# Eight of 32 value parts computed inside the attention steps, and setup work moved off the head of a differential-attention and mixture-of-experts kernel

## What is computed

```python
Q, K = xn @ Wq + bq, xn @ Wk + bk          # 16 heads, two halves of 64 each
V = xn @ Wv + bv                           # 16 heads x 64 = 1024 columns
P = softmax(Q1 K1^T / 8) - lam * softmax(Q2 K2^T / 8)
Y = concat(P V) @ Wo + bo                  # then a layer norm with gamma, beta, times 0.2
main = gelu(xn @ W1m + b1m) @ W2m + b2m    # the shared expert
# routing: per batch, the mean token picks the top 2 of 8 experts
ffn = a * main + (1 - a) * sum(gate_k * expert_k(xn))
```

## Time and profile before

| | |
|---|---|
| median of 3 runs | 1177.49 us (1175.26 to 1177.57) |
| the profiled execution's own time | 1176.92 us |
| its span in the trace | 1175.1 us |
| PE / DVE / ACT / POOL busy | 1128.0 / 904.8 / 949.8 / 979.9 us |
| mean granted TensorE clock | 0.991 of full speed |

### The profile page before, as it was taken

The page is one execution under the profiler, slowest core; times in us unless marked ns, Lnnn a source line. Parts: engine busy times, 40 slices in busy tenths (PEclk is TensorE's granted clock), DMA queues, the critical chain, the costliest instruction groups (busy, mean ns, idle before and its releaser), DMA issues.

```text
span 1175.1 us, 27816 instructions
## 1 busy us (share of the span) xinstructions
PE 1128.0 (96%) x9730; PEld 779.9 (66%) x9730; DVE 904.8 (77%) x1573; ACT 949.8 (81%) x1711; POOL 979.9 (83%) x609
## 2 busy tenths in 40 slices
PE   5899999999999999999999999999999999998998
PEld 4666666666666666666666666666666666664797
DVE  7878888888888888888888888888888888874510
ACT  3288899888898888898888898888898988885432
POOL 2589999999999999998888999999898888899000
PEclk9999999999999999999999999999999999998999
DMA  8942222222211222122212211222222212100000
GB/s 196 344 115 61 48 63 61 61 61 62 53 42 44 61 61 56 45 78 56 55 46 56 50 35 37 56 56 56 56 56 56 56 45 56 43 5 1 1 19 18
DMA packets 76439, 71.28 MB, mean 61 GB/s; under 512 B 43380, under 2 KB 65396, under 8 KB 76404
## 3 DMA queue, kind: packets, MB, share of 16 engines
q1 hardware_dynamic: 75396, 70.65, 23.1%
q10 hardware_dynamic: 880, 0.19, 0.1%
q0 software_dynamic: 128, 0.01, 0.0%
HBM read 22.59 MB, written 14.68 MB: 32 GB/s over the span
## 4 chain that ended last, share of the span: by engine, by line
PE 63%; ACT 20%; issue 6%; POOL 6%; DVE 4%; ACTq 1%; DMA 0%; DVEq 0%; SPq 0%; POOLq 0%
PE ps L567 20%; PE ps L535 18%; ACT work L753 11%; PE ps L553 10%; PE ps L489 8%; ACT p_mix L753 6%; POOL p_mix L448 3%; PE ps L652 3%; ACT pt L766 3%; PE ps L639 2%; POOL work L445 2%; PE ps L516 1%; DVE small L947 1%; DVE pt L903 1%; ACT small L719 0%
## 5 line engine op out<-in xcount | busy, mean ns | idle before, releaser
L947 DVE TENSOR_REDUCE small<-ps 128x1 f32<-128x1024 f32 x512 | 614.3, 1220 | 168.3 <-PE ps L535 168.3
L448 POOL TENSOR_TENSOR p_mix<-p_mix,work 128x1024 f32<-128x1024 f32 x256 | 608.8, 2378 | 21.4
L766 ACT ACTIVATE pt<-ps 128x512 f32<-128x512 f32 x512 | 306.8, 599 | 131.8 <-PE ps L553 129.7
L553 PE MATMUL ps<-ident,p_mix 64*128 64x64 f32 x4096 | 353.1, 227 | 5.6 <-POOL p_mix L448 2.8
L445 POOL TENSOR_SCALAR work<-work,small 128x1024 f32<-128x1024 f32 x256 | 307.4, 1201 | 50.4 <-DVE small L972 48.3
L553 PEld LDWEIGHTS ps<-ident,p_mix 64*128 64x128 f32 x4096 | 305.6, 139 | 55.9 <-issue 37.2
L753 ACT ACTIVATE p_mix<-ps,small 128x1024 f32<-128x1024 f32 x256 | 286.5, 1119 | 16.7 <-DVE small L947 16.7
L753 ACT ACTIVATE work<-ps,small 128x1024 f32<-128x1024 f32 x256 | 285.1, 1114 | 0.1
L567 PE MATMUL ps<-pt,v_h 128*64 128x512 f32 x1024 | 250.2, 610 | 0.7 <-ACT pt L766 0.7
L535 PE MATMUL ps<-k_hi,q_hi 64*128 64x512 f32 x512 | 227.5, 444 | 5.9 <-ACT p_mix L753 3.4
L535 PE MATMUL ps<-k_hi,q_lo 64*128 64x512 f32 x512 | 225.8, 441 | 0.0
(11 more groups left out here) (135 smaller groups left out, 1211.0 us busy)
## 6 DMA issues: line engine op xcount, KB each, us to landing
qx_hi<-q_hi SPq DMA_DIRECT2D x64, 256.0 KB, 3.8
qx_lo<-q_lo SPq DMA_DIRECT2D x64, 256.0 KB, 4.6
v_scratch<-pt SPq DMA_DIRECT2D x16, 512.0 KB, 5.4
v_h<-v_scratch SPq DMA_DIRECT2D x32, 256.0 KB, 3.1
w_scratch<-wqk_hi SPq DMA_DIRECT2D x16, 160.0 KB, 1.8
w_scratch<-wqk_lo SPq DMA_DIRECT2D x16, 160.0 KB, 1.9
wqk_hi<-w_scratch SPq DMA_DIRECT2D x16, 160.0 KB, 2.2
wqk_lo<-w_scratch SPq DMA_DIRECT2D x16, 160.0 KB, 2.3
```

Of the source, the lines that this page charges most:

```text
L448: pool.tensor_tensor(e1, e1, e2, ALU.add).then_inc(mix_done, 1)
L553: mm = pe.transpose(pt_ps[:, c * D:(c + 1) * D], p_mix[rows, col:col + P], ident[rows, rows])
L766: act.activation(pt4[:, kb % 2, :, j * P + half * D:j * P + (half + 1) * D], pt_ps.rearrange("p (c q) -> p c q", c=KC), ACT.Copy).then_inc ...
L947: dve.tensor_reduce(neg_max[:, m:m + 1], slot[SLOT[k, s]], AX.X, ALU.max, negate=True)\
```

## The change

It computes 24 value parts in the head and the last eight in attention steps 0, 1, 2, 4 and 5. Of the 24, every fourth (u % 4 = 3, six parts) is copied by ACT, and POOL adds the bias in SBUF. Parts 0 and 1 are computed ahead of the second `turn_x`. The wait on `v_stored` is split: step 3 waits for tiles 0 to 3 and 8 to 11, step 7 for tiles 4 to 7 and 12 to 15. SP issues `load_v(0, 0, 0)` after tile 11, the store of tile 15 after `prepare(1)`, and the expert weights after `prepare(2)`. `set_main` moves to POOL's steps 129, 130, 132, 133, 137 and 138. `start_y` moves behind `split_w(1)`. In steps 0 to 7 the reciprocals come ahead of the second row maximum.

```diff
+MAIN_AT, INPUT_AT = 129, (132, 133, 137, 138)
+V_LATE = {0: (24, 25), 1: (26, 27), 2: (28, 29), 4: (30,), 5: (31,)}
+V_EARLY = 24
...
+        def by_act(u):
+            return u < V_EARLY and u % 4 == 3
+        def v_out(u):
+            count = sum(by_act(w) == by_act(u) for w in range(u + 1))
+            return (v_copied if by_act(u) else v_evac), count
+        def v_place(u):
+            if u < V_EARLY + 2:
+                return 4 + (u + 2) % 4
+            return 6 if u in (26, 28) else 7
...
-            for i in range(NT):
-                sp.wait_ge(v_evac, 2 * i + 2)
+            def store_v(i):
+                for u in (2 * i, 2 * i + 1):
+                    if by_act(u):
+                        sp.wait_ge(v_added, u // 4 + 1)
+                    else:
+                        sp.wait_ge(*v_out(u))
                 sp.dma_start(v_scratch[i, :, :], v_st[:, i % TB, :]).then_inc(v_stored[i % TB], 16)
+
+            for i in range(V_EARLY // 2):
+                store_v(i)
                 if i % 2 and i // 2 < NW:
                     store_w(i // 2)
                     load_w(i // 2 + 2)
...
             for v in v_stored:
-                sp.wait_ge(v, 16 * B)
+                sp.wait_ge(v, 16)
             load_v(0, 0, 0)
+            for i in range(V_EARLY // 2, NT - 1):
+                store_v(i)
+            def load_experts():
...
             for n in range(1, IT):
                 prepare(n)
+                if n == 1:
+                    store_v(NT - 1)
+                if n == 2:
+                    load_experts()
+                if n == IT // B - 2:
+                    for v in v_stored:
+                        sp.wait_ge(v, 16 * B)
...
-            start_y()
             for n in range(1, NW):
                 split_w(n)
-            set_main()
+            pool.wait_ge(xn_ready, 2 * B)
+            start_y()
+            def bias_v(first, end):
+                for u in range(first, end, 4):
+                    pool.wait_ge(*v_out(u))
+                    hv = u % 2
+                    pool.tensor_tensor(v_part(u), v_part(u), bv_bc[:, hv * BANK:(hv + 1) * BANK], ALU.add)\
+                        .then_inc(v_added, 1)
+            bias_v(3, V_EARLY)
...
+                set_main(n)
                 set_expert(n)
...
-            pe.wait_ge(v_evac, 2 * NT)
...
+                    if isinstance(g, int) and g * BODY + k == LAG:
+                        pe.wait_ge(*v_out(28))
...
+                    if isinstance(blk, int) and blk == 0:
+                        pe.wait_ge(*v_out(2 * NT - 1))
...
+                    if isinstance(g, int) and (g, k) == (0, 1):
+                        pe.wait_ge(*v_out(V_EARLY - 2))
+                        pe.wait_ge(*v_out(V_EARLY - 1))
...
+                if isinstance(g, int) and g == 0:
+                    for u in V_LATE.get(k, ()):
+                        values(u)
...
+                if isinstance(n, int) and (n, w) == (1, 1):
+                    act.wait_ge(v_mm, 2 * NT)
...
-                if half == 0 and isinstance(g, int) and g * BODY + k == LAG:
-                    for v in v_stored:
+                if half == 0 and isinstance(g, int) and g * BODY + k in (LAG, LAG + QB):
+                    for v in v_stored[kb * QB:(kb + 1) * QB]:
                         act.wait_ge(v, 16 * B)
...
-            evac_v(20, 2 * NT)
+            evac_v(20, V_EARLY)
...
-                if j == 1 and now(g, k, 1):
+                soon = isinstance(g, int) and g == 0 and k < TB
+                if (j == 1 or soon and j != 3) and now(g, k, 1):
                     inv_sums()
...
-                if j in (0, 2) and now(g, k, 1):
+                if j in (0, 2) and not soon and now(g, k, 1):
                     inv_sums()
+                if isinstance(g, int) and g == 0:
+                    for u in V_LATE.get(k, ()):
+                        evac_v(u, u + 1)
```

More of the change, by code:

```diff
@@ L144, in build @@
         wv_split, v_mm, v_evac = sem("wv_split"), sem("v_mm"), sem("v_evac")
+        v_copied, v_added = sem("v_copied"), sem("v_added")
         v_stored = [sem(f"v_stored{i}") for i in range(TB)]
@@ L203, in slot_free, with v_free, v_part, v_bank @@
             return exp_done, 2 * (g * BODY + k) + what + 1
+        def by_act(u):
+            return u < V_EARLY and u % 4 == 3
+        def v_free(u):
+            return max([w for w in range(u) if v_place(w) == v_place(u)], default=None)
+        def v_out(u):
[5 more added lines that the diff above has]
+            return 6 if u in (26, 28) else 7
+        def v_part(u):
+            i, hv = divmod(u, 2)
+            return v_st[:, i % TB, hv * BANK:(hv + 1) * BANK]
+        def v_bank(u):
+            return ps[:, v_place(u) * BANK:(v_place(u) + 1) * BANK]
         def xt_bank(i):
@@ L370, in _, with set_main @@
             bias = b2_bc[:, :].rearrange("p (s e) -> p s e", s=SETS)
[L372 to L389, removed]
+            def set_main(n):
+                if n == MAIN_AT:
+                    pool.wait_ge(route, 14)
+                    pool.tensor_copy(coef[:, 0:1], a_mix).then_inc(set_step, 1)
+                    pool.tensor_scalar(gb_bc[:, 0:2 * E], gb_bc[:, 0:2 * E], OUT_SCALE, one, ALU.mult, ALU.mult)\
+                        .then_inc(set_step, 1)
+                    pool.wait_ge(main_loaded, 64)
+                    pool.wait_ge(set_step, 1)
+                    pool.tensor_scalar(bias[:, 0, :], bias[:, 0, :], coef[:, 0:1], one, ALU.mult, ALU.mult)\
+                        .then_inc(set_step, 1)
+                if n == MAIN_AT + 1:
+                    pool.tensor_scalar(w2[:, 0:HC * E], w2[:, 0:HC * E], coef[:, 0:1], one, ALU.mult, ALU.mult)\
+                        .then_inc(set_step, 1)
+                    pool.wait_ge(set_step, 3)
+                    pool.tensor_tensor(bias[:, 0, :], bias[:, 0, :], gb_bc[:, E:2 * E], ALU.add).then_inc(set_step, 1)
+                if n in INPUT_AT:
+                    part = INPUT_AT.index(n)
+                    pool.wait_ge(set_step, 5)
+                    add_row(bias[:, 0, :], part * TB // 2, (part + 1) * TB // 2)
             def add_row(row, t0, t1):
@@ L496, in _, with values @@
             proj(0, 0, 32, 1, slot[2])
-            turn_x(1)
[L500 to L516, removed]
-                                       w[:, hv * BANK:(hv + 1) * BANK], start=j == 0, stop=j == 2)
-                    mm.then_inc(v_mm, 1)
-            pe.wait_ge(v_evac, 2 * NT)
+            def values(u):
+                i, hv = divmod(u, 2)
+                if u == 2:
+                    pe.wait_ge(lo_done, 2)
+                if u % 8 == 0:
+                    pe.wait_ge(xt_lo, i // 4 + 1)
+                if v_free(u) is not None:
+                    pe.wait_ge(*v_out(v_free(u)))
+                for j, (a, w) in enumerate(((xT_hi, wv_hi), (xT_lo, wv_hi), (xT_hi, wv_lo))):
+                    mm = pe.matmul(v_bank(u), a[:, i * P:(i + 1) * P],
+                                   w[:, hv * BANK:(hv + 1) * BANK], start=j == 0, stop=j == 2)
+                mm.then_inc(v_mm, 1)
+            pe.wait_ge(wv_split, 2)
+            values(0)
+            values(1)
+            turn_x(1)
+            for u in range(2, V_EARLY):
+                if u == 14:
+                    pe.wait_ge(route, 2)
+                    pe.wait_ge(small_loaded, 64)
+                    pe.matmul(ps[0:B, 2 * BANK:2 * BANK + NEXP], mean_tok, wg, start=True, stop=True)\
+                        .then_inc(route_mm, 1)
+                values(u)
             def open_scores(g, k, s):
@@ L739, in _, with copy_v @@
             high_x(3)
+            def copy_v(u):
+                act.wait_ge(v_mm, u + 1)
+                after(act, v_stored[u // 2 % TB], 16 * (u // 2 // TB))
+                act.activation(v_part(u), v_bank(u), ACT.Copy).then_inc(v_copied, 1)
+            for u in range(3, 16, 4):
+                copy_v(u)
             act.wait_ge(route, 5)
             act.activation(prob, logit, ACT.Exp, bias=lg_max, scale=1.0, accum_out=lg_sum).then_inc(route_act, 1)
+            for u in range(19, V_EARLY, 4):
+                copy_v(u)
             def exps(g, k, s):
@@ L898, in evac_v @@
                     i, hv = divmod(u, 2)
-                    bank = 4 + (u + 2) % 4
+                    if by_act(u):
+                        continue
                     dve.wait_ge(v_mm, u + 1)
```

31 lines of the change are left out of this document (15 added, 16 removed).

## The result

The changed kernel takes 1186.08 us (median of 4 executions, 1185.49 to 1187.61) against 1177.53 us before (1175.26 to 1178.16): 8.55 us or 0.76% slower, ratio 1.0076, 95% interval 1.0059 to 1.0093.

What follows compares the result with a forecast made beforehand. PE was taken to bound the kernel, busy 1128 of 1175 us, with time to win only in the head and steps 0 to 4. Terms 9.2 + 1.6 + 2.4 = 13.2 on 1176.9 gave 1190.1, stated as 1190.3, range 1183 to 1196.

Steps and rivals of the forecast that it cites:

- The store of tile 15: Steps 7 and 8: the store waits behind POOL's split, so ACT's copy and PE's turning come late, +9.2 us.
- POOL's item 3: POOL's mixing: item 3 starts at 62.8, 3.1 us earlier than before, so tile 15 is issued at 81.9.
- SP's weight transfers: Head: 3.8 us of transfers after tile 1 and 3.7 after tile 3 delay the stores behind them.
- half of the microsecond: Steps 3 to 4: a kept clock could gain a microsecond; half was taken, so step 4 opens at 61.3.
- The head's waits: Head: SP waits about 7 us for POOL before tile 1, DVE for landed tiles; step 0 opens at 44.4.
- the condition: Head: the forecast is wrong if the first row maximum comes before 42 or after 47.
- The clock behind the stall: After PE's hole of nearly 10 us: a lowered clock costs +1.6 us, bounds 0 and 3.2.
- The second batch: Steps 129 to 138: POOL's 7.8 us for the shared expert make PE wait, +2.4 us, bounds 0 and 4.5.
- Edits at nothing: Parts 0 and 1 moved, new PE and ACT waits, late expert loads and store check: cost or give nothing.
- Parts 0 and 1 ahead of the turning: Head: they fill a hole of PE but win nothing, since DVE still begins at 24.75.
- The last addition: 13.2 us on the profiled 1176.9 gives 1190.1; that execution is 0.6 below the median; written as 1190.3.

Runs made afterwards that it cites:

- experiment 1: The changed kernel with the store of value tile 15 issued inside the preparation of head 1, ahead of the store of head 2's weights: 1174.28 us, ratio 0.9981.
- experiment 4: The kernel before, all values in the head, with only the late store of tile 15 and ACT's split wait on the stores: 1193.09 us, ratio 1.0134.
- experiment 9: The kernel before with only POOL's fill of y moved behind the weight split of head 1 and the second half's normalising: 1175.66 us, ratio 0.9988.
- experiment 2: On experiment 1, the preparation of the shared expert spread over POOL's steps 115, 119, 123, 127, 131 and 135: 1171.04 us, ratio 0.9955.
- experiment 3: The kernel before with only the preparation of the shared expert moved from the head to steps 129 to 138: 1178.79 us, ratio 1.0035.
- experiment 7: On experiment 2, value parts 0 and 1 put back behind the second turning of x: 1172.15 us, ratio 0.9956.
- experiment 12: On experiment 11, value parts 0 and 1 put ahead of the second turning of x again: 1170.16 us, ratio 0.9937.
- experiment 6: On experiment 2, POOL fills y behind the six bias additions instead of ahead of them: 1170.69 us, ratio 0.9940.
- experiment 11: On experiment 10, SP's weight transfers of heads 0 and 1 moved behind tiles 10 and 11: 1168.63 us, ratio 0.9935.
- experiment 10: Experiment 2 with the edits of experiment 6 and experiment 7 both: 1168.72 us, ratio 0.9925.

## Why the prediction was right, and where its sizes were off

Forecast 1190.3 (1183 to 1196), measured 1186.08: the sign, the place and the mechanism held, and the size of the loss was overstated, 13.2 us for 10.7 in the profiled executions and 8.55 in the medians.

- **"The store of tile 15. This sets the result."** Right, and shown both ways: taking it out gives back 11.8 us (experiment 1), putting it alone into the kernel before costs 16.8, of which 12.1 stand at the place (experiment 4). The term was **+9.2** and measured **+6.05** (PE's turning at 82.99 for 76.94). This is the step that was mis-sized. Not the chain from POOL's item 3 to the landing: it was 82.73 - 65.93 = 16.8 us to the end of the split and 85.03 + 3.5 - 82.73 = 5.8 more to the landing by my figures, and took 76.42 - 59.64 = 16.8 and 5.8. Off was its start, item 3 at 59.64 where I had put 62.8.
- **Where those 3.2 us were.** 2.0 of them lie ahead of step 0, which opened at 42.40 and not at 44.4, and 1.2 between it and step 4 (58.13 for 61.3). Three inputs were off. First, I priced the moved fill of y at nothing by not pricing it; it held a DVE instruction for over a microsecond, and experiment 9 shows 1.4 us at the first maximum for it alone, 1.15 of them in that instruction. The Trainium skill (SBUF — State Buffer, SBUF: two separate sides) describes an exclusive lock on the port pair that DVE and GpSimd share, held for the whole instruction, which a DVE instruction with two inputs in SBUF meets beside a GpSimd one that reads SBUF; the two rows that end within 0.01 us of each other agree, and I could have read them in the trace of before. Second, SP's weight transfers took 2.8 us (33.60 to 36.37) instead of 3.8; some of that was lost again, since tile 2, issued at 36.48, held DVE until 40.60, 4.1 us and not 3.5. Third, I took half of the microsecond that a full clock would give in steps 3 and 4; the clock stayed at 1.00 there, and step 4 opened 4.05 us after step 3 where I had 4.5. The other 0.7 us are spread over steps 0 to 2, each a little shorter than I had it; DVE did not wait for tile 4, for which I had given 0.4.
- **The head's waits.** SP waited 7.0 us for POOL ahead of tile 1, as forecast, and DVE for tile 2, though only 0.59 us. Step 0 opened at 42.40, inside the 42 to 47 that I had named as the condition.
- **The clock behind the stall.** Forecast +1.6; from PE's restart to the first copy the lag grew from 6.05 to 8.67, +2.6, of which 0.5 came back by copy 1: +2.1 net. The size is that of one execution; the other three ran with a higher mean clock and took 1.5 to 2.1 us less; with the 0.6 by which the profiled execution of before lies below its median, that is where medians and profile part.
- **The second batch.** Forecast +2.4, measured +1.9, shown apart by experiments 2 and 3. My sum took twelve items in a row; the waits came at three places.
- **Edits at nothing.** The reordered reciprocals and the expert loads cost nothing that a run shows. Parts 0 and 1 ahead of the turning cost nothing at step 0 in the change as made (42.32 without them ahead, 42.18 with, experiments 7 and 2), but the reason that I gave was wrong: I said DVE's start bounds the head, but DVE stood 1.03, 0.59 and 0.67 us for PE between 25 and 30 us, with the clock at 0.50 up to 26.
- **The last addition.** The terms give 1190.1 on the profiled execution; with the 0.6 by which it lies below the median the sum is 1190.7, and I wrote 1190.3.

## What to carry to other kernels

When a store or a wait is moved in a queue, read what the instructions ahead of it in that queue wait for: a single issue behind the wrong wait ate 5 us of gain and 6 more. Put added work where an engine already waits, as seen in its idle rows, and the same work was free here. And where two bounds cover each other, test their edits together before discarding either.

## What was not expected of the hardware

- A DVE instruction over 8 columns took 1.32 us while POOL copied 2048 columns and ended with it, against 0.17 us (experiment 9). Another, L1022 of the changed kernel over one column, took 1.27 us beside POOL's bias addition, which started 0.03 us ahead of it:

```profile
38.18 1.27 DVE L1022 TENSOR_TENSOR small<-small 2x1 f32<-2x1 f32 x1
```

```profile
38.15 1.29 POOL L500 TENSOR_TENSOR pt<-pt,o_t 128x512 f32<-128x512 f32 x1 [1.25 <-ACT pt L824]
```

- The clock can differ after the same holes. In the head PE ran at 0.50 after standing 1.85 us in the change and in experiments 2 and 12, and at 1.00 after the same 1.85 us in experiment 6; a hole of 2.30 us in experiment 11 did not bring it down, one of 2.46 us in before did. In the steps the PE rows of experiments 6 and 10 are alike from 49 us up to a hole of 1.47 us that ends at 54.37, and only in experiment 6 the clock fell behind it. Such a fall cost about 1.25 us at the first copy (experiment 6 against 10, and before against 9 beyond the 1.4 that the fill gives). So a difference of one to two microseconds between single traces can be the clock's, whatever the edit. What decides it is left open.
